# A table of its own for the last expert's rows, added in SBUF by the loads, and a finish in halves on VectorE

## What is computed

```python
xn = _layernorm(x, axis=-1)
s = _L1_attn_ref(xn, ...)                       # retention, gated
# the experts, on xf = xn as 4096 rows of 128:
probs = softmax(xf @ router_w.T + router_b)     # two best experts of each token, weights w
toks = xf[tok]                                  # up to 615 tokens for each of 8 experts
h = gelu(einsum('etc,ehc->eth', toks, fc1_w) + fc1_b)
y = einsum('eth,ech->etc', h, fc2_w) + fc2_b
y = toks + y * layer_scale
out = zeros((N, C)).at[tok.reshape(-1)].add((wgt[..., None] * y).reshape(-1, C))
x = x + s * silu(out)
```

## Time and profile before

| | |
|---|---|
| median of 3 runs | 1028.86 us (1028.47 to 1029.36) |
| the profiled execution | 1039.62 us, its span 1037.8 us |
| granted TensorE clock, mean | 0.922 of full speed |
| busy: PE, DVE, ACT, POOL | 885.6 (85%), 823.6 (79%), 724.5 (70%), 263.8 us (25%) |
| moved | 147.19 MB, mean 142 GB/s |

### The profile page before, as it was taken

One profiled execution on the slowest core, in us unless ns is written; L12 is line 12 of the kernel. 1 busy time (PEld: TensorE's weight loads), 2 busy tenths in 40 slices (PEclk: granted clock), 3 DMA queues, 4 the chain that ended last, 5 costly groups with the idle time before them and its releaser, 6 DMA issues. The chain is left out here.

```text
span 1037.8 us, 25027 instructions
## 1 busy us (share of the span) xinstructions
PE 885.6 (85%) x9373; PEld 468.3 (45%) x9374; DVE 823.6 (79%) x1698; ACT 724.5 (70%) x1489; POOL 263.8 (25%) x246
## 2 busy tenths in 40 slices
PE   3999897999999999999898898778998998799940
PEld 3666542333333333333334676533444444377830
DVE  6665497999999999999823765579999999737875
ACT  2666316888888888888774544467999999867731
POOL 4865300000000000000003666400444442014543
PEclk9999759999999999999989888678999999989985
DMA  4679778533333453230004899693454542556716
GB/s 162 228 264 345 244 148 207 166 65 67 72 66 85 93 117 84 64 68 14 12 25 122 294 338 279 208 231 72 97 112 79 103 87 47 133 175 175 254 50 224
DMA packets 133143, 147.19 MB, mean 142 GB/s; under 512 B 19149, under 2 KB 94490, under 8 KB 132384
## 3 DMA queue, kind: packets, MB, share of 16 engines
q1 hardware_dynamic: 129696, 140.60, 49.7%
q0 software_dynamic: 3328, 4.99, 1.7%
HBM read 77.63 MB, written 69.54 MB: 142 GB/s over the span
## 5 line engine op out<-in xcount | busy, mean ns | idle before, releaser
L839 ACT ACTIVATE probsB<-psB 128x512 f32<-128x512 f32 (+2 forms) x640 | 309.9, 565 | 100.4 <-PE psB L913 78.8
L776 DVE TENSOR_REDUCE mxB<-psB 128x1 f32<-128x512 f32 (+2 forms) x448 | 259.6, 644 | 9.4 <-PE psB L884 8.6
L906 PE MATMUL psB<-q_groups,k_groups 64*128 64x512 bf16 (+3 forms) x768 | 209.1, 333 | 29.4 <-ACT probsB L839 19.5
L877 PE MATMUL psB<-k_groups,q_groups 64*128 64x512 bf16 (+3 forms) x768 | 219.8, 343 | 3.0 <-PEq L293 1.7
L944 PE MATMUL psB<-probsB,vB 128*32 128x512 f32 (+3 forms) x1536 | 166.6, 506 | 0.5 <-ACT probsB L839 0.5
L1709 ACT ACTIVATE psD<-psD 128x896 f32<-128x896 f32 (+2 forms) x192 | 153.4, 799 | 16.7 <-PE psD L1763 16.2
L906 PEld LDWEIGHTS psB<-q_groups,k_groups 64*128 64x128 bf16 x768 | 67.4, 94 | 186.4 <-ACT probsB L839 162.5
L1640 DVE TENSOR_REDUCE sumsD<-psD 128x1 f32<-128x128 f32 (+3 forms) x256 | 113.5, 483 | 13.3 <-PE psD L1786 11.3
L884 PE MATMUL psB<-hideB,chooseB 64*128 64x128 bf16 (+1 forms) x1024 | 117.3, 210 | 0.0
L776 DVE TENSOR_REDUCE mx2B<-psB 128x1 f32<-128x384 f32 (+2 forms) x192 | 105.4, 596 | 13.6 <-PE psB L884 11.8
L1763 PE MATMUL psD<-k_groups,q_groups 64*128 64x512 bf16 (+3 forms) x384 | 104.0, 343 | 12.4 <-ACT psD L1709 3.6
(11 more groups left out here) (219 smaller groups left out, 1490.9 us busy)
## 6 DMA issues: line engine op xcount, KB each, us to landing
v<-vaugA SPq DMA_DIRECT2D x4, 2048.0 KB, 8.9
vB<-v SPq DMA_DIRECT2D x16, 512.0 KB
q_groups<-q SPq DMA_DIRECT2D x32, 200.0 KB
k_groups<-k SPq DMA_DIRECT2D x32, 200.0 KB
q_groups<-q SPq DMA_DIRECT2D x32, 192.0 KB
k_groups<-k SPq DMA_DIRECT2D x32, 192.0 KB
back<-emptyB SPq DMA_DIRECT2D x16, 256.0 KB, 4.2
o<-outB SPq DMA_DIRECT2D x128, 32.0 KB, 1.9
```

Source lines behind the costliest of these rows:

```text
L776: nc.vector.tensor_reduce(dst, src, AX.X, ALU.max).then_inc(max_read, 1)
L839: nc.scalar.activation(probs[:, n % DEEP, 0:w], st[n % BANKS][:, 0:w], ACT.Exp, scale=DH ** -0.5).then_inc(exp_done, 1)
L877: ins = nc.tensor.matmul(bank[:, to:to + w], q[half[r], s, hq // 2, t * P:t * P + P], k[half[r], s, hq // 2, HALF * c:HALF * c + w], start ...
L906: ins = nc.tensor.matmul(bank[:, to:to + w], k[half[r], s, hq // 2, jt * P:jt * P + P], q[half[r], s, hq // 2, i0:i0 + w], start=True, sto ...
```

## The change

Three things are changed.

- **A table for the last expert.** Experts 0 to 6 scatter into back as before. Expert 7 scatters into a new table, late, of 4096 rows (a token has it at most once), by a row number from which 4096 is taken where it is 4096 or more; an empty slot's number lies past the end and is not written. late is cleared by eight more transfers of 256 KB behind those of back. SP loads the joined rows when experts 0 to 6 are scattered. VectorE joins batches 0 and 1, then does the last expert, then joins batches 2 and 3 and gates the retention of batch 3. GpSimd waits for the last expert's scatters and issues four transfers (512 KB each) that add late's rows to the joined rows in SBUF. The first two and the last two share a semaphore, and ScalarE waits for both of a pair.
- **The last expert tile by tile.** TensorE puts its five tiles of fc2 products in five PSUM banks and signals each; VectorE does bias, scale and weighting one tile after the other. TensorE waits once more, for VectorE's reading of the last turned retention (banks 0, 1 and 5).
- **The finish in halves, on VectorE.** Silu, the product, the addition of x1 and the store are done for four of the eight tokens of a partition at a time; the additions on GpSimd are gone.

```diff
--- before.py
+++ after.py
@@ -172,7 +172,7 @@
     def wait_slots(self, engine):
-        engine.wait_ge(self.slots_cleared, 16 * (NE + 2 * NTILES // 4))
+        engine.wait_ge(self.slots_cleared, 16 * (NE + 3 * NTILES // 4))
@@ -711,6 +711,9 @@
                                  empty[:, :, :]).then_inc(slots_cleared, 16)
                 for g in range(2 * NTILES // 4):
                     sp.dma_start(A["back"][g * 4 * P:(g + 1) * 4 * P, :].rearrange("(t p) c -> p t c", p=P),
+                                 empty[:, 0:4, 0:D]).then_inc(slots_cleared, 16)
+                for g in range(NTILES // 4):
+                    sp.dma_start(A["late"][g * 4 * P:(g + 1) * 4 * P, :].rearrange("(t p) c -> p t c", p=P),
                                  empty[:, 0:4, 0:D]).then_inc(slots_cleared, 16)
                 for x in range(NQ):
                     if x == 1:
@@ -1861,6 +1864,7 @@
         turned_bank = ps[:, 0:2, :].rearrange("p b f -> p (b f)")
+        last_at = [ps[:, bank, 0:P] for bank in (6, 7, 0, 1, 5)]
@@ -1876,7 +1880,7 @@
         gated, x1 = m.sb("gatedE", [P, B, NT, D]), m.sb("x1E", [P, B, NT, D])
-        rows = [t[:, :, :, :].rearrange("p s a f -> p (s a f)").bitcast(F32).rearrange("p (b t c) -> p b t c", b=B, t=NT)
+        moe, prod = [t[:, :, :, :].rearrange("p s a f -> p (s a f)").bitcast(F32).rearrange("p (b t c) -> p b t c", b=B, t=NT)
@@ -1884,12 +1888,15 @@
         y_biased, y_scaled, shared_ready, z_ready = (m.sem(n) for n in ("y_biasedE", "y_scaledE", "shared_readyE", "z_readyE"))
-        sent = [m.sem(f"sentE{i}") for i in range(2)]
+        sent, late_sent = [m.sem(f"sentE{i}") for i in range(2)], m.sem("late_sentE")
+        late_to, late_step = m.sb("late_toE", [P, SLOT_TILES]), m.sem("late_stepE")
...
         rows_before = [16 * 4, 16 * 3, 16 * 2, 16 * 5 * 2]
-        moe_ready, silued, prod_ready, done, stored = (m.sem(n) for n in ("moe_readyE", "siluedE", "prod_readyE", "doneE", "storedE"))
+        late_in = [m.sem(f"late_inE{i}") for i in range(2)]
+        fours = [slice(0, 4), slice(4, NT)]
+        joined, silued, prod_ready, done, stored = (m.sem(n) for n in ("joinedE", "siluedE", "prod_readyE", "doneE", "storedE"))
@@ -1906,7 +1913,7 @@
                         back = A["back"][kk * N + b * S:kk * N + (b + 1) * S, :]
-                        sp.dma_start(rows[kk][:, b], back.rearrange("(p t) c -> p t c", p=P)).then_inc(rows_in[b], 16)
+                        sp.dma_start((moe, prod)[kk][:, b], back.rearrange("(p t) c -> p t c", p=P)).then_inc(rows_in[b], 16)
@@ -1923,27 +1930,34 @@
                             sp.dma_start(x1[:, b], A["x1"][b].rearrange("p (t c) -> p t c", c=D)).then_inc(x1_loaded, 16)
-                for i in range(2):
-                    sp.wait_ge(sent[i], SENT * (NE // 2))
+                sp.wait_ge(sent[0], SENT * 4)
+                sp.wait_ge(sent[1], SENT * 3)
...
                 for b in range(B):
-                    sp.wait_ge(done, b + 1)
-                    sp.dma_start(A["out"][b].rearrange("(t p) c -> p t c", p=P), res[:, b]).then_inc(stored, 16)
-                sp.wait_ge(stored, 16 * B)
+                    for half, t4 in enumerate(fours):
+                        sp.wait_ge(done, 2 * b + half + 1)
+                        sp.dma_start(A["out"][b, 4 * P * half:4 * P * half + 4 * P].rearrange("(t p) c -> p t c", p=P),
+                                     res[:, b, t4, :]).then_inc(stored, 16)
+                sp.wait_ge(stored, 16 * 2 * B)
...
             def _(pool):
-                for e in range(NE):
+                for e in range(NE - 1):
...
                                                 oob_is_err=False).then_inc(sent[e % 2], 16)
-                pool.wait_ge(x1_loaded, 16 * B)
-                for b in range(B - 1):
-                    pool.wait_ge(prod_ready, b + 1)
-                    nc.gpsimd.tensor_tensor(res[:, b], rows[1][:, b], x1[:, b], ALU.add).then_inc(done, 1)
+                for t in range(SLOT_TILES):
+                    pool.wait_ge(z_ready, SLOT_TILES * (NE - 1) + t + 1)
+                    pool.indirect_dma_start(A["late"], bass.IndirectOffsetOnAxis(ap=to[:, 1, t:t + 1], axis=0),
+                                            z[:, 1, t, :], None, bounds_check=N - 1, oob_is_err=False).then_inc(late_sent, 16)
+                pool.wait_ge(late_sent, SENT)
+                for b in range(B):
+                    pool.wait_ge(joined, b + 1)
+                    pool.dma_start(moe[:, b], A["late"][b * S:(b + 1) * S, :].rearrange("(p t) c -> p t c", p=P),
+                                   accum_op=ALU.add).then_inc(late_in[b // 2], 16)
@@ -1987,11 +2001,13 @@
                         pe.wait_ge(y_biased, 2 * e)
+                    if e == NE - 1:
+                        pe.wait_ge(ret_read, 2 * B)
                     for t in range(SLOT_TILES):
+                        at = last_at[t] if e == NE - 1 else ps[:, 6 + t // 4, (t % 4) * P:(t % 4) * P + P]
                         for c in range(FC):
-                            ins = nc.tensor.matmul(ps[:, 6 + t // 4, (t % 4) * P:(t % 4) * P + P], hT[:, c, t * P:t * P + P],
-                                                   fc2[:, i, c, :], start=(c == 0), stop=(c == FC - 1))
-                        if t in (3, SLOT_TILES - 1):
+                            ins = nc.tensor.matmul(at, hT[:, c, t * P:t * P + P], fc2[:, i, c, :], start=(c == 0), stop=(c == FC - 1))
+                        if t in (3, SLOT_TILES - 1) or e == NE - 1:
@@ -2027,10 +2043,11 @@
                 for b in range(B):
-                    act.wait_ge(moe_ready, b + 1)
+                    act.wait_ge(late_in[b // 2], 32)
                     if b >= 2:
-                        act.wait_ge(prod_ready, b - 1)
-                    nc.scalar.activation(gate[:, b % 2], rows[0][:, b], ACT.Silu).then_inc(silued, 1)
+                        act.wait_ge(prod_ready, 2 * b - 2)
+                    for t4 in fours:
+                        nc.scalar.activation(gate[:, b % 2, t4, :], moe[:, b, t4, :], ACT.Silu).then_inc(silued, 1)
@@ -2128,7 +2145,31 @@
-                for e in range(NE):
+                def last_expert():
+                    e = NE - 1
+                    i, at, first = e % BUFS, e % 2, 2 * e
+                    dve.wait_ge(w_in[i], WEIGHTS * (e // BUFS + 1))
+                    dve.wait_ge(sent[at], SENT * (e // 2))
+                    V.tensor_scalar(late_to[:, :], x[:, i, :, D + 1], float(N), -float(N), ALU.is_ge, ALU.mult).then_inc(late_step, 1)
+                    dve.wait_ge(late_step, 1)
+                    V.tensor_tensor(to[:, at, :], late_to[:, :], x[:, i, :, D + 1], ALU.add)
+                    dve.wait_ge(shared_ready, e + 1)
+                    dve.wait_ge(y_scaled, 2 * e)
+                    dve.wait_ge(z_ready, SLOT_TILES * e)
+                    for t in range(SLOT_TILES):
+                        dve.wait_ge(y_done, first + t + 1)
+                        V.tensor_tensor(y[:, t, :], last_at[t], b2[:, i, :], ALU.add).then_inc(y_biased, 1)
+                        dve.wait_ge(y_biased, first + t + 1)
+                        V.tensor_tensor(scaled[:, t, :], y[:, t, :], ls[:, i, :], ALU.mult).then_inc(y_scaled, 1)
+                        dve.wait_ge(y_scaled, first + t + 1)
+                        V.scalar_tensor_tensor(z[:, at, t, :], scaled[:, t, :], x[:, i, t, D:D + 1], shared[:, at, t, :],
+                                               ALU.mult, ALU.add).then_inc(z_ready, 1)
+
+                def join(b):
+                    dve.wait_ge(rows_in[b], rows_before[b] + 32)
+                    V.tensor_tensor(moe[:, b], moe[:, b], prod[:, b], ALU.add).then_inc(joined, 1)
+
+                for e in range(NE - 1):
@@ -2143,25 +2184,25 @@
                         gate_retention(b)
-
-                def join(b):
-                    dve.wait_ge(rows_in[b], rows_before[b] + 32)
-                    V.tensor_tensor(rows[0][:, b], rows[0][:, b], rows[1][:, b], ALU.add).then_inc(moe_ready, 1)
+                join(0)
+                join(1)
+                last_expert()
+                join(2)
+                join(3)
+                gate_retention(B - 1)
...
                 def result(b):
-                    dve.wait_ge(silued, b + 1)
-                    dve.wait_ge(gated_ready, B)
-                    V.tensor_tensor(rows[1][:, b], gated[:, b], gate[:, b % 2], ALU.mult).then_inc(prod_ready, 1)
-
-                join(0)
+                    dve.wait_ge(gated_ready, b + 1)
+                    for half, t4 in enumerate(fours):
+                        dve.wait_ge(silued, 2 * b + half + 1)
+                        V.tensor_tensor(prod[:, b, t4, :], gated[:, b, t4, :], gate[:, b % 2, t4, :], ALU.mult).then_inc(prod_ready, 1)
+                    for half, t4 in enumerate(fours):
+                        dve.wait_ge(prod_ready, 2 * b + half + 1)
```

(11 more changed lines are left out.)

## The result

The changed kernel takes 1040.77 us (median of 4 runs, 1039.41 to 1045.17), the kernel before 1029.11 us beside it: a ratio of 1.012, with a 95% interval of 1.0088 to 1.0152, or 11.7 us.

What follows compares the result with a forecast made beforehand. It took SP's queue to bound the attention stall and a row of handovers, with no engine full, the end; clears 7.2 plus tail 4.7 make 11.9 us on 1028.86, so 1040.8 us, range 1035 to 1046.

Steps and rivals of the forecast that it cites:

- The clears: Attention part: eight added clears in SP's queue delay the placement TensorE waits for, by 8 x 0.90 = 7.2 us.
- case C: Attention part: timed runs drain clears faster than the profiled one, added ones costing 3.4 us; 1037.0 us, chance 0.15.
- The clock in the stall: Attention part: TensorE's clock has already fallen to 0.50 in the stall, so a longer stall adds no second fall.
- When the rows leave: Tail: row loads start 8.1 us earlier, but the last expert waits behind join(1); its last scatter starts 11.1 us later.
- The adding transfers: Tail: GpSimd's four adding transfers take twice a plain load's time, 2.66 us for 512 KB.
- the middle value: Tail: 2.66 us per 512 KB adding transfer, between a plain load's 1.33 and the slowest clear's rate, 5.0.
- case B: Tail: adding transfers run as fast as plain loads, so the kernel takes 1037.9 us; chance 0.17.
- case D: Tail: adding transfers run at the slowest clear's rate, 5.0 us for 512 KB; 1050.4 us, chance 0.10.
- The finish: End of the kernel: 5.7 us from batch 3's pair landing to VectorE's end, then 3.5 us to the span's end.
- The tail's sum: End of the kernel: the tail ends at 1042.5, 4.7 us later than before.
- From the profile to the median: Whole kernel: the timed median lies 10.8 us below the profiled execution, the same after the change as before.
- Case E: Tail: joins of batches 0 and 1 don't hold VectorE up; 1026.8 to 1029.7 us, chance 0.05.

Runs made afterwards that it cites:

- e10: The changed kernel with VectorE doing the last expert ahead of the joins and all 32 clears issued by GpSimd; 1.0091 of the kernel before.
- e8: The kernel before, unchanged, run again for a second profile; 1.0005 of the kernel before.
- e11: The kernel before with only the finish in halves, the additions of x1 on VectorE instead of GpSimd; 0.9966 of the kernel before.
- e3: The changed kernel with VectorE doing the last expert ahead of the joins of batches 0 and 1; 1.0025 of the kernel before.
- e1: The kernel before with only the new table's eight clears added, behind those of back; 1.0074 of the kernel before.
- e2: The changed kernel with the new table's eight clears issued one at a time behind the loads of the first eight groups; 1.0045 of the kernel before.
- e6: The kernel before with its own 24 clears spread, three behind the loads of each of the first eight groups; 1.0042 of the kernel before.
- e7: The changed kernel with the last expert ahead of the joins and all 32 clears spread behind the first eight groups' loads; 0.9998 of the kernel before.

## Why the prediction was right, and where it was not

- **The clears.** Forecast 8 x 0.90 = 7.2 us on the path; the eight are 0.97 us apart, the wait grew by 6.3 and 7.0 us in the two pairs of profiles, and alone they cost 7.6 us in the timed runs. The step holds. Its wording was too narrow (e10), and of case C's spare time nothing is to be seen. The wait came to 11.1 and 10.2 us, where about 12 was forecast.
- **The clock in the stall.** The prediction said that a longer stall adds no second fall, and in the first pair that holds: the granted clock is at 0.50 (1.2 of 2.4 GHz) from 177 to 183 before and from 178 to 187 after, and back at 1.00 some 4 us after TensorE goes on in both (179.12 and 184.22). It isn't a fixed property of the kernel before: in e8, which waits 3.2 us, the clock stays at 1.00 from 172 to 189, and in e11, which waits 2.8, it falls to 0.50 from 177 to 179.
- **When the rows leave.** Forecast 8.1 us earlier for the row loads; measured from the products' start, 6.4 us instead of 15.3, so 8.9. Join(1) came after 13.9 us instead of the forecast 15.4: 0.8 us of that is the earlier issue, and 0.8 that its rows were in 7.5 us after the first issue and not 8.25. The last scatter starts 22.7 us after the products' start, 9.7 us later than before, where 11.1 were forecast.
- **The adding transfers.** Forecast 2.66 us for 512 KB, measured 2.50. Of the term that was most in doubt the middle value was right; case B (a plain load's pace) and case D (5.0 us) are out.
- **The finish.** Forecast 5.7 us from the last pair's landing to VectorE's end; measured 5.6 us, from ScalarE's start at 1034.71 to VectorE's end at 1039.05 + 1.29 = 1040.34. The last half's store took 3.1 us to the end of the span, not 3.5.
- **The tail's sum.** Forecast 4.7 us; 3.4 us in the first pair of profiles and 4.5 in the second.
- **From the profile to the median.** Here a step failed without harm. The prediction put the same 10.8 us between profile and median on both sides. The changed kernel's profiled execution lay 4.4 us above its median, and the second ones 2.1 and 1.8 us. Parts that no experiment touches differ by as much from one execution to the next: on one chip VectorE's masking in the retention part (first to last) took 226.6, 228.9, 233.7 and 234.3 us in four kernels. So two spans, one of each kernel, told 5.6 us, and the parts by themselves told 6.3 + 3.4 = 9.7.
- **Case E** went out with VectorE's wait of 9.30 us, and e3 showed its gain to be real in another order: 7.8 to 8.4 us of the tail.

1040.77 against 1040.8 is closer than the terms deserve, and the last tenths are luck: the clears came out 0.4 us dearer in e1, the tail a little cheaper, and neither is known to better than 2 us from the timed runs.

## What to carry to other kernels

Before a burst of bulk transfers is made longer, look in the profile for the small transfer behind it that an engine waits for: here eight clears of a table that is used some 840 us later cost 7.6 us, more than the 4.6 us that the change lost at the end (e2). Where they stood is what cost: one at a time behind the groups' loads they cost nothing that could be measured (e2), while spreading all of them, three or four to a group, brought new waits (e6 and e7), and another issuing engine brought a longer one (e10). An engine that works in order must do the work that others wait for ahead of the work that waits for a transfer. And an adding transfer took 1.75 times a plain one here, with the DMA engines as busy; what it saves VectorE has to be set against that. Test the parts of a change one by one: the finish in halves was worth having by itself, the table was not. The last expert tile by tile was never run without the table; in e3 the last scatter starts 10.75 us after the products' start (999.37 - 988.62) instead of 13.03 before, which speaks for it.

## What was not expected of the hardware

- TensorE had to wait 17.3 us for two transfers of 8 KB beside the clears that GpSimd had issued (e10), although they came from another queue.
- Clearing in pieces of 2 KB instead of 512 bytes shortened 8.9 MB of clears only from 34.3 to 27.9 us.
- The part of the experts takes 71.1 us in some executions and 73.2 to 74.4 in others, and the retention part differs by up to 8.7 us between profiles (225.6 to 234.3), with the same instructions. What decides it was not found.
